# Moving the first read of the projection weight behind the scan loop

## What is computed

```python
# layer 0, block 1: a gated linear recurrence over time (written in logs in the reference)
xn = layernorm(x)
k  = xn @ Wz + bz ; g = xn @ Wh + bh
h[t] = sigmoid(-k) * h[t-1] + sigmoid(k) * tilde(g)      # a scan along t
x  = x + (layernorm(h) * gamma + beta + xn)

# layer 0, block 2: feed-forward with fake-quantized weights and a low-rank addition
def fake_quant_weight(w, bits=8):
    scale = max(abs(w)) / 127                             # one maximum over the whole matrix
    return clip(round(w / scale), -128, 127) * scale
h = gelu(layernorm(x) @ fake_quant_weight(W_fc).T + lora_fc)
x = x + h @ fake_quant_weight(W_proj).T + lora_proj
```

## Time and profile before

| | us |
|---|---|
| median of 2 timed runs | 3145.64 (3142.52 to 3148.77) |
| the profiled execution | 3176.29 |
| its span on the slowest core (core 1) | 3174.7 |
| spans of the eight cores | 3121.1 to 3174.7 |

### The profile page before, as it was taken

How to read it: one execution, slowest core, us unless ns; L and a number is a source line. 1 busy time by engine, 2 the same in 40 slices (tenths; PEclk the granted TensorE clock), 3 DMA queues, 4 the chain that set the end, 5 groups by cost and what they waited for, 6 DMA issues and landing times.

```text
span 3174.7 us, 23200 instructions; the slowest of 8 cores (3121.1 to 3174.7 us)
## 1 busy us (share of the span) xinstructions
PE 1477.3 (47%) x7364; PEld 739.9 (23%) x7364; DVE 1428.9 (45%) x1701; ACT 630.4 (20%) x826; POOL 242.9 (8%) x156
## 2 busy tenths in 40 slices
PE   3055523040132077878888863135415544130984
PEld 0021100000111055645555540012102211000331
DVE  3866667888999910000000003764584521025222
ACT  0033320000111012332233210015404400160002
POOL 0300000303000000000000000240040000132000
PEclk9986655555565588987777885567758877555997
DMA  7223330410433300000000037110010023723016
GB/s 173 80 80 106 119 107 17 141 41 0 96 106 107 106 27 25 10 21 27 27 6 22 27 52 165 47 40 1 0 40 1 0 73 96 149 93 106 1 33 167
DMA packets 86039, 201.14 MB, mean 63 GB/s; under 512 B 13424, under 2 KB 29808, under 8 KB 83104
## 3 DMA queue, kind: packets, MB, share of 16 engines
q1 hardware_dynamic: 69168, 165.77, 17.8%
q0 software_dynamic: 14736, 19.20, 4.1%
q10 hardware_dynamic: 2016, 14.68, 1.2%
HBM read 178.97 MB, written 39.85 MB: 69 GB/s over the span
## 4 chain that ended last, share of the span: by engine, by line
DVE 35%; PE 25%; DMA 18%; ACT 11%; issue 8%; POOL 1%; SPq 1%; DVEq 1%; ACTq 0%; POOLq 0%
PE PB L38 25%; DVE SC L38 13%; DVE X L38 8%; DMA E<-SP 7%; DVE E L38 5%; ACT L38 5%; DMA SC<-SP 4%; DVE XB L38 3%; DVE H L38 3%; ACT SC L38 2%; ACT X L38 2%; DVE AT L38 2%; DMA E<-WPRT 2%; DMA AT<-SP 2%; DVE MX L38 2%
## 5 line engine op out<-in xcount | busy, mean ns | idle before, releaser
L38 ACT ACT_TABLE_LOAD x223 | 286.1, 1283 | 2529.7 <-PE PB L38 1251.8
L38 PE MATMUL PB<-XB,X 128*128 128x256 bf16 (+1 forms) x2304 | 370.0, 313 | 303.2 <-DVE X L38 118.8
L38 PE MATMUL PB<-E,H 128*128 128x256 bf16 (+1 forms) x2176 | 311.2, 309 | 201.7 <-DVE H L38 133.3
L38 DVE TENSOR_SCALAR SC<-PB,QS,SMT 128x256 f32<-128x256 f32 x64 | 34.8, 544 | 742.3 <-PE PB L38 534.4
L38 PE MATMUL PB<-XB,H 128*128 128x512 bf16 x896 | 248.7, 441 | 252.4 <-DVE X L38 142.7
L38 PEld LDWEIGHTS PB<-XB,X 128*128 128x128 bf16 x2304 | 222.2, 105 | 411.4 <-issue 328.6
L38 PE MATMUL PB<-X,H 128*128 128x512 bf16 x512 | 145.4, 454 | 327.0 <-ACT SC L38 116.9
L38 PE MATMUL PB<-SC,ONESB 128*128 128x512 bf16 x320 | 161.9, 608 | 291.4 <-DVE SC L38 178.0
L38 PEld LDWEIGHTS PB<-E,H 128*128 128x128 bf16 x2176 | 226.3, 107 | 277.8 <-issue 231.2
L38 PEld LDWEIGHTS PB<-XB,H 128*128 128x128 bf16 x896 | 94.1, 109 | 407.2 <-issue 370.5
L38 PEld LDWEIGHTS PB<-X,H 128*128 128x128 bf16 x512 | 56.7, 113 | 416.1 <-issue 378.5
(11 more groups left out here) (132 smaller groups left out, 1880.7 us busy)
## 6 DMA issues: line engine op xcount, KB each, us to landing
AT<-WFCT SPq DMA_DIRECT2D x32, 512.0 KB, 4.1
E<-WFCT SPq DMA_DIRECT2D x32, 512.0 KB, 4.5
AT<-WPRT SPq DMA_DIRECT2D x32, 512.0 KB, 3.4
E<-WPRT SPq DMA_DIRECT2D x32, 512.0 KB, 3.4
AT<-SP SPq DMA_DIRECT2D x32, 512.0 KB, 3.7
E<-SP SPq DMA_DIRECT2D x32, 512.0 KB, 3.7
E<-SP SPq DMA_DIRECT2D x56, 256.0 KB, 5.6
X<-XT SPq DMA_DIRECT2D x2, 4096.0 KB, 32.1
```

The source lines that it names most:

```text
L38: ins = f(*args, **kw)
```

## The change

`p1pr` is made and emitted in one piece after the scales of WFCT, and not within the loop; the loop emits 8 chunks of WFCT for each m instead of 4 and 4. `Pass1` gets an argument `gate`, which its body doesn't use. Since WFCT has 32 chunks and 4 come before the loop, the loop's bursts are then 8, 8, 8 and 4 chunks behind scans 0 to 3 and nothing behind scans 4 to 7. The memset of WPRT's column of MX moves along. The number of loads and of reductions is the same.

```diff
         class Pass1:
-            def __init__(self, hbm, nrows, ping):
+            def __init__(self, hbm, nrows, ping, gate=None):
                 self.hbm = hbm
...
         p1fc = Pass1(WFCT, KT, 8)
-        p1pr = Pass1(WPRT, 32, 10)
         p1fc.emit(4)
...
             k.V(scan)
-            p1fc.emit(4)
-            p1pr.emit(4)
+            p1fc.emit(8)
         p1fc.emit(64)
-        p1pr.emit(64)
         mloop_T = ("tensor", k.snap("tensor"))
...
         f_fc, f_fc_tok = p1fc.fin()
         qfc_tok = pass1_fin(f_fc, 0, 7, f_fc_tok)
+        p1pr = Pass1(WPRT, 32, 10, gate=f_fc_tok)
+        p1pr.emit(64)
 
         lnh_rows = ln_stats(lambda kk, n: HD[kk][:, n * NSZ:(n + 1) * NSZ],
```

## The result

| | us | against before |
|---|---|---|
| before, median of 38 runs | 3155.36 (3138.16 to 3221.32) | |
| changed, median of 39 runs | 3171.95 (3156.93 to 3245.79) | ratio 1.0055, 95% interval 1.0041 to 1.0069 |
| span of the changed kernel's profile, core 7 | 3167.1 (cores: 3127.5 to 3167.1) | |

The forecast was 0.5% more, +16.9 us; measured is 0.55% more, about +17 us (0.0055 x 3155), with an interval of +13 to +22. Both ends of it are far from 2%. The absolute 3162.5 us stood on a median of two runs; the kernel before is at 3155.4 in 38 runs, so it is the difference that was forecast well.

A forecast was written before the change was run, and what follows sets the result against it. The prediction took the loop to be one serial queue on VectorE, stretched by a two-slot ring. Its terms, 85.2 + 3.0 - 11.4 - 50.8 - 9.1 = +16.9 us, added to 3145.6 gave 3162.5 us, range 3143 to 3191.

The forecast's parts named there:

- (3): Loop iteration 4, scan 3 to scan 4: four chunks instead of eight, 11.4 us saved.
- (4): Loop iterations 5 to 7, without bursts: ScalarE sets 20.3 us each instead of 37.23, 50.8 us saved.
- Step (2): Loop iterations 1 to 3: three gaps waiting for WFCT instead of one, 3.0 us more in all.
- Step (6): New tail behind scan 7: 16 pairs of WPRT chunks and the memset, 85.2 us, hidden by nothing.
- G: Gap for two WPRT chunks in series, in bursts and tail: taken as 5.39 us, possibly 4.92 to 5.89.
- Shifted, not changed: From HD's LayerNorm statistics on, every stage is only shifted; time behind HD's first cast changes by a few us at most.
- Rival A: The WPRT tail behind the loop streams better than the bursts, no load late: sum -17 us, 3128 us; chance 8%.
- Rival B: The WPRT tail streams worse with all eight cores reading: sum +120 us, 3266 us; chance 4%.
- Rival D: Order doesn't matter, chunks cost the same wherever they stand in VectorE's serial queue: 3146 us; chance 10%.
- Rival E: Loop iterations 5 to 7 don't shrink at all, for a reason no row shows: +68 us, 3213; chance 2%.
- Rival C: TensorE becomes the bound of loop iterations 5 to 7: sum +34 to +45 us, 3180 to 3191 us; chance 12%.

The follow-up runs named there:

- e9: The changed kernel itself, run again: ratio 1.0058 (1.0039 to 1.0078) to the kernel before, +18 us.
- e1: The changed kernel with all 60 chunks left after the first four emitted behind the loop: ratio 1.0142 to the kernel before, +45 us.
- e3: The kernel before without WPRT's first read, W_proj's scale taken from W_fc's maximum: ratio 0.9722 to the kernel before, -88 us.
- e5: The kernel before with six slots instead of two for the first reads: ratio 0.9802 to the kernel before, -62 us.
- e8: The kernel before with chunks spread in pairs behind the scan and the first three tiles' evictions, six slots: ratio 0.9764 to the kernel before, -74 us.
- e6: The changed kernel with six slots instead of two for the first reads: ratio 0.9869 to the kernel before, -41 us.
- e7: The kernel before with chunks spread in pairs behind the scan and the first three tiles' evictions, two slots: ratio 0.9819 to the kernel before, -57 us.
- e10: The changed kernel without WPRT's first read, run a second time in more rounds: ratio 0.9799 to the kernel before, -63 us.
- e2: The changed kernel without WPRT's first read, W_proj's scale taken from W_fc's maximum, first run: ratio 0.9831 to the kernel before, -53 us.
- e4: The changed kernel with matrices exchanged, WPRT read in the loop and WFCT behind it, first run: ratio 1.0123 to the kernel before, +39 us.
- e12: The changed kernel with matrices exchanged, WPRT in the loop and WFCT behind it, second run: ratio 1.0114 to the kernel before, +36 us.

## Why the prediction was right

- **The bound.** That the loop is one queue on VectorE, stretched by loads, held: six slots take the waits for loads out of the iteration and nothing else, a spread order shortens it by what ScalarE leaves open.
- **Steps (3) and (4)** were within 0.5 us. The floor of 20.3 was added up from ScalarE's rows of the kernel before, in which it never ran without a burst; it came out at 20.31.
- **Step (2)** was too low by 2 us: gaps that wait for WFCT are 6.09 us in the mean of the cores, where one iteration of one core gave 5.89. Over all cores of the kernel before the same mean is 6.03, and 28 of its 56 gaps are below 5.9: the row that I used was a middle one, but single gaps of up to 7.1 us raise the mean, and a sum of gaps needs the mean. The gaps make 4.3 of the measured 4.9 us; the other 0.6 is the time from the last AT reduction to the first eviction, which was taken as unchanged.
- **Step (6)** was too high by about 2 us: G is 5.27 instead of 5.39. Steady reading isn't slower than bursts.
- **Shifted, not changed.** Up to the cast the sum is 16.9 in the profiles and the whole moved by +17. The timed runs bear it out within 3 us for the changed kernel (e9 too), e1, e3, e5 and e8; e6, e7 and e10 were 5 to 7 us above their shift, e2, e4 and e12 9 to 13. Each profile is one execution, and the shift of its cast and the median of other executions needn't agree to a few us; none of the larger differences goes the other way, so a small return behind the cast stays open for those. The profiles give the time behind the cast itself (a core's span less the start of its first cast, mean of the cores): 2661.6 us in the changed kernel and 2663.1 in e9, against 2662.7 on cores 4 to 7 of the kernel before, whose cores 0 to 3 took 2690.2 at granted clocks of 0.69 to 0.72. Two executions of one kernel differ there by more than the return that is asked for: 2671.5 and 2656.6 (e2, e10), 2674.2 and 2654.9 (e4, e12). So the profiles show no return in the changed kernel, but a single one can't show a return of less than some 15 us; the timed runs, +17 (13 to 22) and +18 (12 to 25), are the closer measure.
- **Rival A** (a faster tail) fell in the changed kernel, since two slots can't do it; e6 shows what it takes. **Rival B** fell in e6. **Rival D** fell in e1. **Rival E** had nothing for it: the iterations shrank. (B and E add up to 6%, not to the 5% that the prediction gives for slower.)
- **Rival C** (TensorE becomes the bound of iterations 5 to 7) was given the highest chance of the rivals, on a price from the wrong core. I had it at 4.73 us for a group, with 1.4 us to spare in an iteration; it ran at 3.61 and 0.37 between groups, a granted clock of 1.00 in the stretch shown. The 4.73 was read on core 1 of the kernel before. Its cores 2 to 7 ran the same groups at 3.61 already, which leaves 20.3 - 4 x 3.98 = 4.4 us (core 7's rows are in the last section). So the 12% for C rested on a core that six of the eight don't bear out.

In short: a burst in the loop costs about 5 us less than the same chunks of WPRT behind it (16.9 us for three and a half bursts). 4.2 of these are ScalarE's evictions that run under it (21.1 us of burst lengthen an iteration by 16.9), and the rest, 5.27 - 4.48 = 0.8 us, is that its first two chunks have landed while VectorE was busy with something else, so a burst of four pairs has three gaps. With WFCT in the tail too it is more, 46 us for seven bursts in e1, since its gaps are the longer ones.

## What to carry to other kernels

Work that fills waits on an engine's queue isn't a sum: price a moved block at both places, once by what the queue gets shorter and once by what it gets longer, and look for what other engines do under it at the old one. A block of small loads and short instructions is best spread, a pair at a time, over the points where its engine waits anyway; here that was worth 57 us with no added buffer, where gathering the same block cost 17 to 45. Where each instruction waits for its own load at a DMA share well below one, count the slots and not the bytes.

## What the runs showed that I had not expected

- TensorE's granted clock differs between the cores of one execution, and the earlier trace rows show one of the two slow ones. In the kernel before, cores 0 and 1 took 4.36 us for 16 matmuls at 0.81 (nearly every dense group from 187 us on); cores 2 to 7, two of them on the same die, took 3.61 at 1.00, the upper of the two levels (2.4 GHz), with the same bursts in the loop. These are core 7's rows for the stretch of the earlier trace rows:

```profile
193.56 3.61 PE L38 MATMUL PB<-XB,H 128*128 128x512 bf16 x16 [0.37 <-DVE SC L38]
...
192.00:196.70 4.70, 4.33 (x21) 1.84 (x20) 3.69 (x4) 0.45 (x1) 0.00 (x0) 1.00 0.00 0
```

  In the changed kernel all eight cores take 3.61 for a group, but for first ones after a pause (4.9 to 6.5 us), in iterations with bursts and without. So the 3.61 on core 7 isn't an effect of the change. Why cores 0 and 1 were lower in that one execution is open.
- The same 512 KB land in 3.4 us from WPRT and 4.2 from WFCT, and the difference follows the matrix wherever it is read. A row of DMA sizes doesn't show this; the gap between pairs does, 5.3 against 6.1 us. The rule that the prediction laid beside G (the Trainium skill, "DMA: Bandwidth & Descriptors", section "Anatomy of one DMA", an estimated 3.2 us) is near to WPRT's 3.4 and doesn't give WFCT's 4.2. That section states its fit for loads issued by GpSimd, which the prediction left out; the loads here are issued by SyncE.
